# Round one of the expert layer closes one pair of positions earlier, and its first groups move between the projections of pairs 6 and 5

## The reference, cut to what matters

```python
h = einsum('bg,egp->bep', x, weight * mask) + bias        # x 64x5000; weight 16x5000x128: 64 batches, 16 positions
h = h + attention(layernorm(h))                           # 8 heads, causal over the 16 positions, small projections
h = h + ffn(layernorm(h))

def ffn(x):                                               # 1024 tokens of 128
    top_scores, top_idx = top_k(sigmoid(x @ gate_w.T), 2) # 64 experts, each token takes two
    ...                                                   # scores normed, times 2.5
    h = silu(buf @ w1) * (buf @ w3); y = h @ w2           # per expert, 128 -> 64 -> 128
    shared = silu(x @ sw1) * (x @ sw3) @ sw2
    return shared + sum of the two y, weighted
```

## Time and profile before

| | |
|---|---|
| median of 3 runs | 241.35 us (240.23 to 242.11) |
| the profiled execution | 241.4 us, of which 239.7 us is the span from first to last instruction |
| PE / DVE / POOL / ACT busy | 184.3 / 152.4 / 145.6 / 82.7 us |
| DMA | 65.12 MB, mean 272 GB/s over the span |
| mean granted TensorE clock | 0.953 of full speed |

### The profile page before, as it was taken

One profiled execution on the slowest core, in us unless ns is written; L12 is line 12 of the kernel. 1 busy time (PEld: TensorE's weight loads), 2 busy tenths in 40 slices (PEclk: granted clock), 3 DMA queues, 4 the chain that ended last, 5 costly groups with the idle time before them and its releaser, 6 DMA issues.

```text
span 239.7 us, 6216 instructions
## 1 busy us (share of the span) xinstructions
PE 184.3 (77%) x2549; PEld 154.8 (65%) x2549; DVE 152.4 (64%) x366; ACT 82.7 (35%) x245; POOL 145.6 (61%) x117
## 2 busy tenths in 40 slices
PE   0057969558989969979879789699997989999700
PEld 0056949457878958857758767588776767767400
DVE  0024384686497796897996994978999627410571
ACT  2005200003324324324133124136878744344400
POOL 3326469519998949879969949620161651375360
PEclk9999997977999989999999999999999999999975
DMA  6989999999999999999999999949901329234241
GB/s 220 290 311 417 362 419 384 346 421 415 421 413 417 420 418 420 414 427 418 403 408 228 234 218 191 153 87 303 263 0 44 115 68 296 68 98 121 71 112 35
DMA packets 32982, 65.12 MB, mean 272 GB/s; under 512 B 2874, under 2 KB 25367, under 8 KB 32375
## 3 DMA queue, kind: packets, MB, share of 16 engines
q1 hardware_dynamic: 31416, 59.47, 75.0%
q10 hardware_dynamic: 576, 3.26, 3.4%
q0 software_dynamic: 960, 1.97, 3.1%
HBM read 56.96 MB, written 7.73 MB: 270 GB/s over the span
## 4 chain that ended last, share of the span: by engine, by line
PE 32%; DVE 24%; DMA 18%; SPq 9%; ACT 6%; issue 5%; POOL 3%; POOLq 1%; DVEq 0%; ACTq 0%
DMA ring<-in_L_tok_weight_dram 16%; PE bank L843 10%; DVE ring L1241 5%; SPq L362 4%; DVE bank L1271 4%; PE bank L1045 3%; DVE prod L1262 3%; PE bank L1015 3%; DVE prod L1293 2%; DVE bank L1301 2%; SPq L368 2%; PE bank L993 2%; PE bank L999 2%; PE bank L928 2%; POOL rstd L455 2%
## 5 line engine op out<-in xcount | busy, mean ns | idle before, releaser
L466 POOL TENSOR_TENSOR ring<-ring,mask 128x896 f32<-128x896 f32 (+1 forms) x48 | 91.5, 1935 | 18.7 <-DMA ring<-in_L_tok_weight_dram 18.6
L843 PE MATMUL bank<-ring,xT 128*64 128x128 f32 x1248 | 84.3, 294 | 11.3 <-DVE ring L1241 8.0
L843 PEld LDWEIGHTS bank<-ring,xT 128*64 128x64 f32 x1248 | 76.4, 149 | 16.0 <-DVE ring L1241 12.8
L1241 DVE TENSOR_TENSOR ring<-ring,bank 128x1024 f32<-128x1024 f32 (+1 forms) x45 | 45.8, 1049 | 35.4 <-DMA ring<-in_L_tok_weight_dram 35.4
L455 POOL TENSOR_TENSOR rstd<-mv,half 128x1 f32<-128x1 f32 (+1 forms) x24 | 14.4, 603 | 32.4 <-DVE mv L1249 21.5
L533 POOL DMA_INDIRECT ring<-expert_outputs,slot_index x16 | 16.2, 1010 | 16.6 <-DMA expert_outputs<-ring 12.4
L824 PE MATMUL bank<-cst,w 64*128 64x64 f32 x39 | 5.3, 328 | 15.6 <-DMA w<-in_x_dram 14.8
L486 POOL DMA_INDIRECT expert_inputs<-xf,slot_index x14 | 14.3, 1022 | 4.3 <-issue 3.5
L508 POOL TENSOR_TENSOR mask<-ring,mask 128x256 f32<-128x256 f32 x8 | 7.5, 938 | 14.4 <-ACT ring L705 11.4
L824 PEld LDWEIGHTS bank<-cst,w 64*128 64x128 f32 x39 | 5.0, 219 | 15.7 <-issue 14.8
L579 ACT ACTIVATE offset<-shift,rstd 128x1 f32<-128x1 f32 x16 | 4.7, 292 | 25.1 <-POOL rstd L455 25.1
(11 more groups left out here) (153 smaller groups left out, 297.4 us busy)
## 6 DMA issues: line engine op xcount, KB each, us to landing
ring<-in_L_tok_weight_dram SPq DMA_DIRECT2D x48, 832.0 KB, 13.5
expert_inputs<-w ACTq DMA_DIRECT2D x3, 1024.0 KB, 10.6
ring<-expert_inputs SPq DMA_DIRECT2D x6, 512.0 KB, 5.4
expert_outputs<-ring SPq DMA_DIRECT2D x12, 256.0 KB, 2.7
mask<-in_L_tok_mask_dram SPq DMA_DIRECT2D x3, 832.0 KB, 15.6
w<-in_x_dram SPq DMA_DIRECT2D x1, 1250.0 KB, 13.0
w2p<-in_L_ffn_w_dram SPq DMA_DIRECT2D x1, 1024.0 KB, 19.2
xT<-masks_dram SPq DMA_DIRECT2D x1, 1024.0 KB, 8.1
```

What stands on the lines that cost most here:

```text
L466: pool.tensor_tensor(unit(j, q, SPLIT(q // 2), UC), unit(j, q, SPLIT(q // 2), UC), mask[:, (m + SPLIT(q // 2)) * D:(m + UC) * D], ALU.mult ...
L843: last = pe.matmul(bank[0][64 * par:64 * par + 64, 0:D], xT[:, (UC * t + c) * B:(UC * t + c + 1) * B], unit(j, 2 * t + par, c, c + 1), sta ...
L1241: dve.tensor_tensor(both(j, t, a, b), both(j, t, a, b), m.rearrange("p (u f) -> p u f", u=1).to_broadcast([P, 2, (b - a) * D]), ALU.mult). ...
```

## The change

`NCH1` becomes 4. Pairs 0 to 3 go to round one and pairs 4 to 7 to round two; sizes of the tables, of the slots and the number of groups stay. Pair 4's gate, rank and slots follow round two's rules, and its gather moves behind the store of round two. `scatter(3)` is issued on POOL at the beginning of stage 7 and `scatter(4)` behind the loop. On SP the three large `load_w2` stand behind the loads of round one's rows. In the tail, `turn_xs(0)`, `turn_xs(1)`, `up(0)`, `up(1)` and `turn_xs(2)` on PE and the three copies on ACT stand between the projections of pair 6 and the output of pair 5, and 16 of 23 `spin` matmuls go.

```diff
-NCH1 = 5
+NCH1 = 4
-SCATTERED = {4: (0,), 5: (1,), 6: (2,), 7: (3,)}
+SCATTERED = {4: (0,), 5: (1,), 6: (2,)}
...
-            load_w2(1, (0, H), (0, PAIRS))
-            load_w2(0, (WREM, H), (0, PAIRS))
-            load_w2(0, (0, WREM), (S, PAIRS))
...
             sp.wait_ge(s_scat[0], 16 * 2 * NCH1)
             for i in range(GROUPS1 // 2):
                 load_slots(0, i)
+            load_w2(1, (0, H), (0, PAIRS))
+            load_w2(0, (WREM, H), (0, PAIRS))
+            load_w2(0, (0, WREM), (S, PAIRS))
             sp.wait_ge(s_tok, 3 * NCH)
...
             for c in range(NCH):
                 b, d = c - 2, c - 3
+                if c == NCH - 1:
+                    scatter(NCH1 - 1)
                 mask_pieces(POOL_SHARE[0])
...
-            scatter(NCH1 - 1)
+            scatter(NCH1)
...
             norm_qk(k)
             score_exp(0, NCH1)
+            copy_xsT(0)
             turned_qk(k)
+            copy_xsT(1)
             heads_k(k)
             norm_h(l)
             copy_oT(j)
             heads_v(k)
             copy_xnT(l)
-            copy_xsT(0)
-            copy_xsT(1)
             square_qk(l)
+            copy_xsT(2)
             norm_qk(l)
             probs(k)
-            copy_xsT(2)
             norm_xf(j)
             copy_xsT(3)
...
-            spin(8, 7)
+            spin(4, 7)
             turn_qk(k)
-            spin(4, 7)
+            turn_xs(0)
             qkv(k)
+            turn_xs(1)
             turn_o(j)
-            spin(3, 7)
+            up(0)
             values(k)
             attend(j)
-            spin(2, 7)
             turn_xn(l)
-            turn_xs(0)
+            up(1)
             project(l)
+            turn_xs(2)
             spin(3, 7)
-            turn_xs(1)
-            spin(3, 7)
-            turn_xs(2)
-            up(0)
-            up(1)
             turn_xs(3)
             turn_qk(l)
             turn_xf(j)
```

## The result

The changed kernel takes 247.08 us (median of 4 runs, 246.06 to 249.51), the kernel before 241.73 us; the ratio is 1.0237 (95% interval 1.0136 to 1.0337). Run again beside the later experiments (e11) it took 245.96 us against 240.75, ratio 1.0202 (1.0152 to 1.0251). A ratio is worked out from the runs that stood side by side, without the few that were over 1.5% slower than the fastest of their kernel, so it isn't quite the quotient of the two medians. By the ratios the changed kernel is slower by 4.9 to 5.7 us. The forecast was 3.8 us.

What follows compares the result with a forecast made beforehand. From 157 us one chain of waits through PE, ACT and DVE, ending in POOL's late gathers, was taken as the bound. Late gathers 2.61 plus tail order 1.19 gave 3.8 us on 241.4, so 245.2 us, range 242.0 to 247.6.

Steps and rivals of the forecast that it cites:

- the forecast's own 244.3 to 246.5: Whole kernel: the prediction's main case for the time after the change, given a 54% chance.
- the clock falls: Rival: between 158 and 164 us PE's clock drops, qkv(6) and two groups' turns cost about 2.2 us, 247.4 us; 5%.
- Part 1: Kernel's end: two more gathers in POOL's late batch, 1.30 us each, reach the end whole, +2.61 us.
- Parts 2 and 3: POOL's scatters and SP's load order: nobody waits longer, cost 0, with 0.45 us to spare on POOL.
- Part 4: Tail's order on PE and ACT: two copies ahead of pair 6's keys delay multiply_keys(6), less four fillers, +1.19 us.
- the twelve other fillers: Tail on PE: the removed fillers beyond the first four, 2.8 us, lay in PE's waits and counted 0.
- A rule against the change: Tail from 157 us: PE busy about 1.9 of 3 us was taken to keep the clock, against the skill's stricter rule.
- granted clock 1.00 from 157 to 170 us: Sign of being right: PE's clock stays at full level through the tail's start, despite the missing fillers.
- PE's list as the bound: Rival: in the tail fillers were real cost, 3.7 us come back against the gathers' 2.6, 240.3 us; 11%.
- Rows late: Rival: group 0's row loads land after 158 us and ACT waits at copy_xsT(0); 248 us at 3 us late; 5%.
- Overflow: Rival: round two's fullest expert exceeds 32 tokens and a 256-pass loop runs, over 500 us more; 4%.

Runs made afterwards that it cites:

- e11: The changed kernel run once more, unchanged, beside the later experiments: 245.96 us against 240.75 for the kernel before, ratio 1.0202.
- e3: The changed kernel with the tail's two lists on PE and ACT as before, so only the gathers, scatters and SP's order changed: 242.88 us, ratio 1.0051.
- e5: The changed kernel with copy_xsT(1) moved behind heads_v(6) on ACT and 16 fillers put back in PE's waits: 242.43 us, ratio 1.0066.
- e7: The kernel before with pair 4's two gathers moved from the early batch to the late one: 243.10 us, ratio 1.0072.
- e9: The kernel before with pair 4's gathers in the late batch, as e7, run once more for its trace: 243.03 us, ratio 1.0064.
- e13: The changed kernel with 24 filler matmuls at PE's very start, while it waits for x: 246.98 us, ratio 1.0257.
- e4: The kernel before with the same 16 fillers taken out and nothing else: 243.88 us, ratio 1.0079.
- e2: The changed kernel with copy_xsT(1) moved on ACT from ahead of heads_k(6) to behind heads_v(6), nothing else: 245.13 us, ratio 1.0134.
- e12: The kernel before run once more, unchanged, for a second trace of its clock and end; the traced execution took 243.22 us.
- e1: The changed kernel with ten fillers back in PE's waits, before qkv(6), turn_xn(7) and turn_xf(5): 245.16 us, ratio 1.0125.

## Why the prediction was right, and where it wasn't

The direction and the range held (247.08 in 242.0 to 247.6), the size was short by 1.1 to 1.9 us, and the sum of 3.8 came from one term that was too large and one that was missing. That the range held is in part luck: 247.08 lies outside the forecast's own 244.3 to 246.5 and beside the 247.4 of the rival "the clock falls", which had 5%; e11's 245.96 lies inside.

*Part 1, two late gathers, +2.61.* The batch grew by 2.74 us, as worked out. That each late gather reaches the end whole is the step that failed in size: by their ratios e3, e5, e7 and e9 measure 1.2, 1.6, 1.7 and 1.5 us, with intervals that lie between 0.4 and 2.5. In the traces of kernels with six late gathers the end takes 18.0 to 18.7 us from the last copy (five traces), with eight 20.0 to 20.3 where the store lands early (six, e13's among them). The difference, about 1.8 us, is the batch's 2.6 less a landing of the store that is shorter by about 0.6 us and of the last gather by about 0.2. The table has the store's part beside the instruction packet's place; why the last gather lands sooner isn't shown.

*Parts 2 and 3, 0.* Right: 0.44 us to spare on POOL for the 0.45 forecast, and SP's rows at 144.19 with nobody waiting. What the prediction didn't see is that the rows were close to the path before the change: in e4 and e9, which have the old order on SP, PE waited 0.84 and 0.70 us for them.

*Part 4, +1.19.* The mechanism was right, copy for copy: 1.39 us at `multiply_keys(6)` in the first trace, 1.10 in e11; e2 takes 0.70 to 0.99 away by moving one copy. That the twelve other fillers count 0 was wrong. If the order's 1.1 to 1.4 us reach the end whole, the 3.3 to 4.5 us that e3 and e5 leave for order and fillers hold another 2 to 3 us (an estimate) that the sum has at nothing.

*"A rule against the change".* This is the step behind the missing term. I took the earlier trace rows, a fall after 0.96 of 3 us busy, as the measure, and judged 1.9 of 3 safe, with 5% for the clock; "granted clock 1.00 from 157 to 170 us", one of its signs of being right, didn't come. In the changed kernel it fell with 2.31 to 2.32 of 3, and after 1.73; e4 took the fillers out alone and lost 1.9 us. The single rows of before at 1.00 didn't show that the kernel before can lose the clock too, as e9 and e12 did. The rule of the Trainium skill (TensorE: Matmul & The Clock Gate, "What's actually happening") that the slow clock is the default and activity lifts it was the better guide, and the trace after agrees with it: 1.00 with the fillers in e5, 0.50 to 0.54 without; that the clock can also fall with the fillers there, as in e9 and e12, isn't in that sentence. The rival's price of 2.2 us was too high for the dip that it meant: of the 2.86 us that `multiply_keys(7)` came later in the changed kernel, filling the first dip (e1) gave 1.4 back (20.16 to 18.75; against e11's 19.55 it is 0.8). The second dip, in 172 to 185 us, wasn't foreseen, so the rival's 247.4 is close to the 247.08 by chance. The norm of pair 6, forecast 1.19 us late, was 4.35 and 2.63 late in the two traces.

*The other rivals.* PE's list as the bound: no, with 16 fillers less the kernel before got slower (e4). Rows late: no, group 0's turns follow `turn_qk(6)` at once. Overflow: no, no trace has the loop. That the last store would land later (4.57 and 5.07 us to the first late gather, 4.11 and 3.82 before) was in none of them.

Together: 1.2 to 1.7 us for the late gathers, and 3.3 to 4.1 us that go when order and fillers are repaired (from e5's 1.0066 to 1.0202 and 1.0237). The two traces of the changed kernel are of executions above its medians (249.51 and 248.18 us); in them the last copy's end is 4.57 and 2.83 us later from `keep_h(7)` than e3's (68.48 and 66.74, 63.91), and from there to the end of the span it is 1.5 and 2.1 us more than in e3 (21.70 and 22.24, 20.18), most of it before the first late gather. How order, clock and landing share the loss in a median execution isn't shown.

## What to carry to other kernels

Filler matmuls in a wait are part of the schedule: who puts real work in their place has to count what stays idle around the new waits, on both sides, and look at more than one execution for the clock. A copy that is moved ahead on an in-order engine costs its own time, and its producer's too where that producer stands behind the work that the engine waits for. And a batch that grows at the end of a kernel is measured by itself (e7) before it is summed.

## What the runs showed of the hardware that I had not expected

- The granted clock fell to its lower level after stretches with PE busy 2.32 and 2.31 of 3 us (changed kernel, 157 to 163 us), where no single wait of its matmuls was over 1.4 us. The busy share by itself doesn't tell: with the same two lists and 2.60 and 2.52 of 3 us busy in 169 to 175 us it stayed at 1.00 in the kernel before and in e3 and fell to 0.50 in e9; the kernel before itself did both in two executions, 241.4 and 243.22 us.
- Where one packet of the instruction queue fell beside a store of 256 KB, the first gather came up to 5.07 us behind the last copy, and 3.19 to 3.35 us where it fell 1.5 us or further off. With 48 more instructions at the start of PE's list (e13, one trace) it came 1 us earlier against the store, and the gather at 3.29 us. That it is the cause isn't shown beyond this.
